# Four-layer block on one core: offsets in chunks of 12 units, the last attention group's rows done early, the recurrence's fillers on both sides of its input products

## What is computed

```
x = x + _L0_conv_ref(_gn(x), ...)   # attention of 8x8 blocks over 14x14 windows, 4 heads
x = x + _L1_conv_ref(_gn(x), ...)   # LSTM of 128 cells along each row's 96 columns
x = x + _L2_conv_ref(_gn(x), ...)   # deformable 3x3 convolution: offsets, gather, weights
x = x + _L3_conv_ref(_gn(x), ...)   # 8x8 block transform M X M^T
```

```
offset = conv2d(x, p_w, p_b, 1, 1)
m = jax.nn.sigmoid(conv2d(x, m_w, m_b, 1, 1))
...
x_off = g_lt * gather(qx_lt, qy_lt) + g_rb * gather(qx_rb, qy_rb) + g_lb * gather(qx_lt, qy_rb) + g_rt * gather(qx_rb, qy_lt)
x_off = x_off * m
return conv2d(x_off, conv_w, None, stride=KS, padding=0)
```

## Time and profile before

| | us |
|---|---|
| median of three executions | 5246.77 (5221.74 to 5258.37) |
| the profiled execution | 5189.45 |
| its span | 5187.6 |
| busy in the span: PE, PEld, DVE, ACT, POOL | 2740.8, 2081.7, 2181.9, 1129.5, 2570.3 |
| image 0: attention, recurrence, offsets | 16 to 262, 262 to 529, 529 to 593 |
| image 1 | 593 to 1148, to 1675, to 1781 |
| image 2 | 1781 to 2312, to 2851, to 2993 |
| image 3 | 2993 to 3529, to 4070, to 4200 |
| transforms and the remaining units | 4200 to 5188 |

### The profile page before, as it was taken

One profiled execution on the slowest core, in us unless ns is written; L12 is line 12 of the kernel. 1 busy time (PEld: TensorE's weight loads), 2 busy tenths in 40 slices (PEclk: granted clock), 3 DMA queues, 4 the chain that ended last, 5 costly groups with the idle time before them and its releaser, 6 DMA issues.

```text
span 5187.6 us, 53724 instructions
## 1 busy us (share of the span) xinstructions
PE 2740.8 (53%) x19674; PEld 2081.7 (40%) x19674; DVE 2181.9 (42%) x4593; ACT 1129.5 (22%) x3009; POOL 2570.3 (50%) x2614
## 2 busy tenths in 40 slices
PE   6889556646665566646555546665655631100102
PEld 4678334435554334435544334444544421100101
DVE  6644445434333555534333454544333442321322
ACT  4544222212222122222222122222222110000000
POOL 1000445445555445545554645544554667677574
PEclk9899766655555656655555656655555655555555
DMA  7410434312111344312111243412111211111111
GB/s 223 119 35 1 125 108 120 98 47 58 36 36 48 110 122 119 100 46 61 36 39 36 88 127 110 129 52 66 36 37 33 93 56 53 51 52 50 37 52 41
DMA packets 192847, 374.01 MB, mean 72 GB/s; under 512 B 59312, under 2 KB 89264, under 8 KB 192576
## 3 DMA queue, kind: packets, MB, share of 16 engines
...
...
## 4 chain that ended last, share of the span: by engine, by line
another core or an unknown queue 27%; DVE 18%; PE 17%; issue 14%; POOL 7%; ACT 4%; DMA 0%; SPq 0%; DVEq 0%; POOLq 0%; ACTq 0%
POOL got L582 7%; PE gates L1441 4%; DVE got L857 4%; DVE red L859 2%; PE bank L1358 2%; PE bank L1251 2%; DVE mx L941 2%; PE gates L1327 1%; PE bank L1302 1%; DVE samp L862 1%; PE gates L1341 1%; ACT tcell L733 1%; PE bank L1292 1%; PE bank L1497 1%
## 5 line engine op out<-in xcount | busy, mean ns | idle before, releaser
L582 POOL DMA_INDIRECT got<-sample_table,index x2592 | 2556.9, 986 | 2554.2 <-DVE red L859 1245.1
L1441 PE MATMUL gates<-hist,whh 128*128 128x96 f32 x3040 | 642.4, 379 | 163.5 <-DVE hist L1111 132.4
L1251 PE MATMUL bank<-turned,wout 128*128 128x96 f32 x1728 | 348.5, 385 | 687.8 <-issue 277.8
L1441 PEld LDWEIGHTS gates<-hist,whh 128*128 128x128 f32 x3040 | 571.0, 281 | 262.2 <-DVE hist L1111 202.5
L1251 PEld LDWEIGHTS bank<-turned,wout 128*128 128x128 f32 x1728 | 334.8, 297 | 704.9 <-DVE turned L866 371.8
L1421 PE MATMUL gates<-xs,wa 128*128 128x192 bf16 (+1 forms) x776 | 252.7, 326 | 492.2 <-ACT sig L731 229.9
L857 DVE TENSOR_TENSOR got<-got,weight 128x1152 f32<-128x1152 f32 x288 | 388.0, 1347 | 260.9 <-DMA got<-sample_table,index 252.4
L941 DVE TENSOR_REDUCE mx<-gates 128x2 f32<-128x392 f32 x576 | 298.9, 556 | 463.6 <-remote 257.0
L1358 PE MATMUL bank<-pt,v 98*18 98x128 f32 x4608 | 287.3, 351 | 186.9 <-issue 143.0
L1103 DVE TENSOR_TENSOR prod<-sig,gc 128x96 f32<-128x96 f32 x384 | 96.3, 251 | 608.4 <-ACT sig L725 359.9
L658 ACT ACTIVATE pt<-gates 98x512 f32<-98x512 f32 x384 | 219.8, 595 | 471.7 <-remote 244.8
...
## 6 DMA issues: line engine op xcount, KB each, us to landing
...
got<-sample_table,index POOLq DMA_INDIRECT x2592
...
```

Of the source, the lines that this page charges most:

```text
L582: pool.indirect_dma_start(out=got[:, uu % RING, n, :], out_offset=None, in_=tables[p], in_offset=bass.IndirectOffsetOnAxis(ap=at, axis=0)) ...
L1251: mm = pe.matmul(out_ps[n % 2][:, at:at + GN], wout[:, tap, :], turned[:, k % 2, tap, :], start=(tap == 0), stop=(tap == NTAP - 1))
L1441: pe.matmul(gate[n][:, h:h + W], whh[:, HID * GATE_OF[n]:HID * (GATE_OF[n] + 1)], hist[:, (t - 1) % HIST, :], start=False, stop=True, skip ...
```

## The change

Eight edits. WARM goes from 10 to 4, and `keep_warm` is called twice in image 0's steps: once ahead of `inputs_ahead` (in every step but the last), once behind it as before. A chunk of offsets has 4 rows (12 units) instead of 8, so there are six chunks, each one group of matmuls in one of two banks, one read by ACT, one run of `pixel_math`; weights and indices have 8 slots of 12 instead of 4 of 24, and the points are as many as before. In the last pass of an attention stage TensorE makes the output rows of the three finished passes (j 0 to 2) in banks 7 and 1, and only those of j = 3 behind the last copy. `add_attention` of the groups before stands two steps later. The memsets of `near` move from `prepare` to the end of `lstm`, so ACT's first rows don't wait for the halo rows; those of `ones` and `gc` move behind the first columns. The first table store is split in two.

```diff
--- before.py
+++ after.py
...
@@ -45,7 +45,7 @@
 GATE_OF = (1, 2, 0, 3)
-WARM = 10
+WARM = 4
 HIST = 16
...
@@ -56,7 +56,7 @@
 TABLE = TROWS * PADW * J
-MROWS = 8
+MROWS = 4
 CH = MROWS * NCOL
...
@@ -65,12 +65,12 @@
 NADD = NGRP // ADDS
-SLOTS2 = 4
+SLOTS2 = 8
 RING = 6
 TURNS = [(r, r + 1) for r in range(1, R + 2, 2)] + [(0,)]
 HIGH_ORDER = [i + 1 - 2 * (i % 2) for i in range(len(TURNS) - 2)] + [len(TURNS) - 2]
 HIGH_AT = {i: n + 1 for n, i in enumerate(HIGH_ORDER)}
-TSTORES = ((1, 9, 4, 6), (9, 17, 8, 10), (17, 24, 12, 12), (24, 26, 13, 13), (0, 1, 14, 13))
+TSTORES = ((1, 4, 2, 2), (4, 9, 4, 6), (9, 17, 8, 10), (17, 24, 12, 12), (24, 26, 13, 13), (0, 1, 14, 13))
...
@@ -153,7 +153,7 @@
 TABLE_POINTS = 4
-PREP_POINTS = TABLE_POINTS + 2 * NCH
+PREP_POINTS = TABLE_POINTS + NCH
 FLUSH = 8
...
@@ -286,6 +286,7 @@
         misc_ps = bank[7]
+        last_ps = (bank[7], bank[1])
         gate = [bank[1 + n][:, 0:2 * W] for n in range(4)]
...
@@ -649,7 +650,8 @@
                     wait(act, x_added, 2 * (GG - 1) + i + 1)
-                    act.activation(sums_in[:, i].rearrange("p k n -> p (k n)"), misc_ps[:, 0:NB * QS], ACT.Copy).then_inc(sums_in_done, 1)
+                    rows = last_ps[i] if G == NG - 1 else misc_ps
+                    act.activation(sums_in[:, i].rearrange("p k n -> p (k n)"), rows[:, 0:NB * QS], ACT.Copy).then_inc(sums_in_done, 1)
...
@@ -754,11 +756,8 @@
                     wait(act, raw_done, n)
-                    for half in range(2):
-                        act.wait_ge(off_done, 2 * n + half + 1)
-                        ins = act.activation(ot[:, CH // 2 * BLK * half:CH // 2 * BLK * (half + 1)], off_ps[half][:, 0:CH // 2 * BLK],
-                                             ACT.Identity, bias=obias[:, 0:1])
-                        ins.then_inc(off_out, 1)
+                    act.wait_ge(off_done, n + 1)
+                    act.activation(ot[:, :], off_ps[m % 2][:, 0:CH * BLK], ACT.Identity, bias=obias[:, 0:1]).then_inc(off_out, 1)
...
@@ -767,12 +766,13 @@
                 normalise()
-                act.wait_ge(near_pads, 4 * (p + 1))
+                act.wait_ge(near_pads, 4 * p + 2)
                 wait(act, tab_stored, 16 * len(TSTORES) * p)
                 for a in range(1, R, 8):
                     near_rows(a, a + 8)
                 for i in range(len(TURNS)):
                     if i == 4:
+                        act.wait_ge(near_pads, 4 * (p + 1))
                         act.wait_ge(halo_in, 32 * (p + 1))
...
@@ -1036,9 +1036,9 @@
                         if G >= 1:
-                            if (b, s) == (1, 0):
+                            if (b, s) == (1, 2):
                                 add_attention(G - 1, 0)
-                            if (b, s) == (1, 2):
+                            if (b, s) == (2, 0):
                                 add_attention(G - 1, 1)
...
@@ -1088,10 +1088,11 @@
                 combine(p, 1, 6)
-                dve.memset(ones[:, :], 1.0).then_inc(bias_ones, 1)
-                dve.memset(gc[:, 1, :], 0.0).then_inc(cell_zero, 1)
                 for k in range(2):
                     columns(k)
+                    if k == 0:
+                        dve.memset(ones[:, :], 1.0).then_inc(bias_ones, 1)
+                        dve.memset(gc[:, 1, :], 0.0).then_inc(cell_zero, 1)
                     rest_part(k)
...
@@ -1119,6 +1120,8 @@
                     point()
+                dve.memset(near[:, :, 0:1], 0.0).then_inc(near_pads, 1)
+                dve.memset(near[:, :, 1 + W:PADW + 1], 0.0).then_inc(near_pads, 1)
                 add_linear(W // LIN - 1)
...
@@ -1138,8 +1141,6 @@
                                   mean[P - C:P, p % 2, 2:3], ALU.mult, ALU.add).then_inc(near_pads, 1)
-                dve.memset(near[:, :, 0:1], 0.0).then_inc(near_pads, 1)
-                dve.memset(near[:, :, 1 + W:PADW + 1], 0.0).then_inc(near_pads, 1)
                 wait(dve, tab_stored, 16 * len(TSTORES) * p)
...
@@ -1147,7 +1148,6 @@
                 for m in range(NCH):
-                    point()
                     pixel_math(p, m)
...
@@ -1165,7 +1165,7 @@
                 flat = gt[:, :, NTAP:NOFF]
-                dve.wait_ge(off_out, 2 * n + 2)
+                dve.wait_ge(off_out, n + 1)
                 if m == 0:
...
@@ -1282,6 +1282,16 @@
 
+                def out_rows(to, i, columns):
+                    N = BLOCK * NB * BLOCK // 2
+                    for k in range(2):
+                        for slot in range(2):
+                            for j in columns:
+                                mm = pe.matmul(to[C * j:C * (j + 1), N * k:N * (k + 1)], hrows[:, i, k, slot, :],
+                                               osb[:, j, :].rearrange("p (t s q) -> p s t q", s=2, q=QS)[:, slot],
+                                               start=(slot == 0), stop=(slot == 1))
+                    return mm
+
                 def project(kind, G, i):
...
@@ -1295,13 +1305,7 @@
                         pe.wait_ge(pv_read, NU * p + J * (G + 1))
-                        N = BLOCK * NB * BLOCK // 2
-                        for k in range(2):
-                            for slot in range(2):
-                                for j in range(J):
-                                    mm = pe.matmul(misc_ps[C * j:C * (j + 1), N * k:N * (k + 1)], hrows[:, i, k, slot, :],
-                                                   osb[:, j, :].rearrange("p (t s q) -> p s t q", s=2, q=QS)[:, slot],
-                                                   start=(slot == 0), stop=(slot == 1))
+                        mm = out_rows(misc_ps, i, range(J))
                     elif kind == "k":
...
@@ -1404,8 +1408,14 @@
                             sums(U, 0)
+                        if U == NU - 1 and s < 2:
+                            if s == 0:
+                                misc_free(MISC_NUMBER["o", NG - 1, 0])
+                                pe.wait_ge(pv_read, NU * (p + 1) - 1)
+                            out_rows(last_ps[s], s, range(J - 1))
+                pe.wait_ge(pv_read, NU * (p + 1))
                 for i in range(2):
-                    project("o", NG - 1, i)
+                    out_rows(last_ps[i], i, range(J - 1, J)).then_inc(misc_done, 1)
...
@@ -1441,7 +1451,7 @@
 
-                def keep_warm(t):
+                def keep_warm():
                     for i in range(WARM):
...
@@ -1464,11 +1474,13 @@
                         recurrence(t)
+                    if p == 0 and t < W - 1:
+                        keep_warm()
                     inputs_ahead(t)
                     if t % LIN == 0 and t > 0:
                         linear(t // LIN - 1)
-                    elif p == 0:
-                        keep_warm(t)
+                    elif p == 0 and t < W - 1:
+                        keep_warm()
                     point()
...
@@ -1490,14 +1502,13 @@
                         pe.wait_ge(taps_in, 16 * (p + 1))
-                    for half in range(2):
-                        wait(pe, off_out, 2 * (n - 1) + half + 1)
-                        for tap in range(NTAP):
-                            top = MROWS * m + MROWS // 2 * half + tap // 3
-                            mm = pe.matmul(off_ps[half][:, 0:CH // 2 * BLK], cw[:, tap, :],
-                                           near[:, top:top + MROWS // 2, tap % 3:tap % 3 + W], start=(tap == 0), stop=(tap == NTAP - 1))
-                        mm.then_inc(off_done, 1)
-                        point()
+                    wait(pe, off_out, n - 1)
+                    for tap in range(NTAP):
+                        top = MROWS * m + tap // 3
+                        mm = pe.matmul(off_ps[m % 2][:, 0:CH * BLK], cw[:, tap, :],
+                                       near[:, top:top + MROWS, tap % 3:tap % 3 + W], start=(tap == 0), stop=(tap == NTAP - 1))
+                    mm.then_inc(off_done, 1)
+                    point()
```

## The result

The changed kernel took 5254.97 us (median of 22 executions, 5241.06 to 5270.32) against 5239.76 us (22 executions) before: ratio 1.0032, 95% interval 1.0020 to 1.0044. It is 15 us slower by the medians and 17 by the ratio, where I had forecast 19.5 us faster. A second series gave 1.0041 (1.0023 to 1.0059). The profiled execution of the changed kernel took 5248.89 us, near its median.

The account below looks back on a forecast made before the run. It took the tail as a fixed block of gathers, with savings only ahead of it: -5.7 - 15 + 2.2 + 2.4 - 3.4 = -19.5 us, carried to the 5246.77 us median as 5227 us; range 5175 to 5275.

Parts of the forecast that it names:

- Chunks of 12, image 0: Image 0's offsets stage: six chunks at 6.9 us instead of larger ones at 10.1, ending at 592.4 instead of 590.1, +2.2 us.
- the first store: Splitting the first table store: one more DMA on SP, the table lands sooner, but image 0's first units are wanted later; 0.
- Chunks, images 1 to 3: Offsets stages of images 1 to 3: three small chunks hidden in the wait for the late fourth group, three behind; +2.4 us.
- Last output rows: Attention ends: moving 48 of 64 recorded output-row matmuls ahead of the last copy saves 15 us over three images, between -39 and +6.
- My sign for this term: Attention ends, images 1 to 3: ACT reads the last sums less than 15 us after the last copy if the term holds.
- Fillers: Image 0's recurrence: four fillers ahead of the input products and four behind save 0.16 us on 36 steps, -5.7 us.
- Memsets: Memsets off the path to the first columns and ACT's first rows no longer behind halo rows and two memsets: -3.4 us.
- quotients: Attention stages: five pairs of add_attention per image move two steps back, nobody waits for them; 0, between -2 and +2 us.
- The tail: From the last offsets to the last gather: a block of fixed length, about 937 us, 878 of them gathers, untouched by the edits.
- the first, that the end of a run sets the time: Rival on the attention ends: they gain nothing, by the page's rule or the gather run's end; -4.5 us, 5242, chance 0.25.
- the late group of images 1 to 3 that comes in time: Rival on the offsets stages: the late group finishes before TensorE slows, saving 3 x 33 = 99 us, 5128; chance 0.13.
- Too few fillers: Rival on image 0's recurrence: eight fillers don't hold the clock, steps take 4.3 instead of 2.66 us, +156 us, 5363; chance 0.05.

## Why the prediction was wrong

The measured time, 5255 us, lies inside my range of 5175 to 5275, but only because the range is wide. The direction was wrong, and two of the five terms of the sum were.

- **Chunks of 12, image 0 (+2.2), with the first store (0): the step that failed.** DVE's chunks take 6.7 to 6.9 us where nothing is late, as forecast (6.9), and there the stage is 1.4 to 1.6 us longer, as forecast. But I costed only DVE's path to the statistics, and put the split store at 0 because nobody wants the first units yet. Together they let POOL's first run begin at 558.8 instead of 565.0, with four of six groups unread instead of three, and with twice as many instructions on DVE for the same pixels, each of which ends in a semaphore. It cost 46 us in the stage; 22 came back, since the run no longer reached into image 1's attention. That the held first gather puts the group back to its rhythm, and that putting back the chunks and the one store removes the loss, is shown. Which of the two would do it alone is not. Nor is it shown why the kernel without the chunks, whose run begins 15.0 us ahead of its sixth read, escapes, and the fifth group here, due 12.6 us behind the run's begin, doesn't; that DVE's instructions come denser is a guess.
- **Chunks, images 1 to 3 (+2.4).** Not seen apart; offsets stages 103.6, 140.0 and 137.1 us against 106.3, 141.7 and 130.4, and up to 140.8 in other profiles without them.
- **Last output rows (-15): not there.** I let the moved matmuls finish ahead of the slow stretch, and forgot that the last copy of sums needs TensorE too: it waits in their place. My sign for this term, the wait between copy and read, fell as if the term were right, since it did not count the wait ahead of the copy. Everything but the chunks came to -4 (-15 to +6) and fillers with memsets to -8 (-17 to +1), so the rows with the later quotients come to +4 us, uncertain by some 14: not the -15 that I took, but the sign stays open. In image 0, without a run, the stretch from the copy to the statistics is 7.4 us: I had 6.7 against 9.1.
- **Fillers (-5.7): right.** 262.5 to 262.9 us in all profiles with them, 268.1 to 268.8 in all without, -5.9 us (the ones' and cell's memsets, 0.2, are in it), at both levels; the clock stayed at 0.97.
- **Memsets (-3.4), quotients (0).** Below what the runs can tell in the total; with the fillers 8 us of 9.1, between 17 and -1.
- **The tail:** 938 us, as said. **The rivals:** the first, that the end of a run sets the time, was true for the attention ends (+4 us, uncertain by 14, where it had 0); the late group of images 1 to 3 that comes in time never came. Too few fillers didn't come either, and its time was added up wrongly: 5227 + 156 is 5383 us, not 5363. A group newly caught in a run, because the run starts earlier, was no rival of mine; the nearest was a longer run in some stage, a half sentence at 0.04. By my own sign (a stage of images 1 to 3 that changes by over 20 us) I was wrong in kind: image 1's attention went from 555 to 534.
- **The page's rule.** At the low level the traces agree with the Trainium skill, "SBUF — State Buffer", section "Who interferes with whom": TensorE's results are on time in an unbroken run of gathers (read 3.0 us behind the copy). At the high level they are not, with the same transfers. The rule speaks of ports of SBUF, and what is held up at the high level includes SP's bare semaphore increments, so the two need not clash. I took the rule as a rival that leaves the gathers out; the held gathers show that they are in it. The Trainium skill, "NOTIFIC — the notification-queue block", section 7.1, has it that the block that records events holds back its producers when its inner queues are full, and counts the stalls, rather than losing a record inside the block. Increments that wait would fit that; records that are missing (150 against 1216) need something more. No run here shows it, since every execution, the timed ones too, was recorded.

**Open:** what puts a chip at the one level or the other; by what way a gather run holds up increments, and TensorE's by 50 us; what chunks or the split store alone do at the high level; whether an unrecorded execution would be late at all; why the chunks cost 7 to 9 us at the low level with 1.6 seen, and why all but the chunks gains 19 us there.
